# Layer 0 values as three fp32r products, key maxima from a block-diagonal kT_hi, loads issued by SyncE, and another order of steps, in a fused two-layer gated cross-attention kernel

## What is computed

```python
x = x + tanh(g_xattn[0]) * L0_xattn(layernorm(x), ctx)   # 16 heads of 64, keys and values from ctx
x = x + tanh(g_ffn[0])   * L0_ffn(layernorm(x))          # softmax gate, 8 experts of 256x256, threshold 0.1
x = x + tanh(g_xattn[1]) * L1_xattn(layernorm(x), ctx)   # 16 heads of 16, biases
x = x + tanh(g_ffn[1])   * L1_ffn(layernorm(x))          # routed swiglu experts
# x: (64, 256, 256), ctx: (64, 120, 256), all float32

def L0_xattn(x, ctx):
    q, k, v = x @ Wq.T, ctx @ Wk.T, ctx @ Wv.T           # inner size 1024
    attn = softmax(q k / 8)                              # per head, 256 queries x 120 keys
    return (attn @ v) @ Wo.T + bo
```

## Time and profile before

| | |
|---|---|
| median of three runs | 3751.11 us (3750.22 to 3751.85) |
| profiled execution, own time | 3753.66 us |
| its span | 3751.7 us |
| TensorE busy | 3675.7 us, 98% |
| TensorE weight loads | 2990.3 us, 80% |
| VectorE busy | 2420.4 us, 65% |
| ScalarE busy | 1707.0 us, 46% |
| GpSimd busy | 1508.2 us, 40% |
| mean granted TensorE clock | 0.997 |

### The profile page before, as it was taken

The page is one execution under the profiler, slowest core; times in us unless marked ns, Lnnn a source line. Parts: engine busy times, 40 slices in busy tenths (PEclk is TensorE's granted clock), DMA queues, the critical chain, the costliest instruction groups (busy, mean ns, idle before and its releaser), DMA issues.

```text
span 3751.7 us, 96179 instructions
## 1 busy us (share of the span) xinstructions
PE 3675.7 (98%) x34836; PEld 2990.3 (80%) x34836; DVE 2420.4 (65%) x5566; ACT 1707.0 (46%) x3115; POOL 1508.2 (40%) x1589
## 2 busy tenths in 40 slices
...
PEclk9999999999999999999999999999999999999999
...
GB/s 96 11 14 16 11 14 16 11 14 16 11 14 16 11 14 16 11 14 16 11 14 16 11 14 16 11 14 16 11 14 16 11 14 16 11 14 16 11 27 64
DMA packets 58916, 64.83 MB, mean 17 GB/s; under 512 B 5344, under 2 KB 55808, under 8 KB 58240
## 3 DMA queue, kind: packets, MB, share of 16 engines
...
## 4 chain that ended last, share of the span: by engine, by line
PE 77%; POOL 7%; DVE 7%; issue 5%; ACT 2%; POOLq 1%; DVEq 1%; SPq 0%; DMA 0%; ACTq 0%
PE g L834 24%; PE g L840 13%; PE scores L834 10%; PE g L987 6%; PE scores L937 6%; POOL q_lo L608 4%; PE g L1006 3%; PE g L903 3%; PE scores L997 3%; DVE y_nm L1269 3%; POOL kmx L601 2%; PE g L854 2%; PE scores L971 2%; PE scores L941 2%; PE g L914 1%
## 5 line engine op out<-in xcount | busy, mean ns | idle before, releaser
L777 ACT ACTIVATE prob<-scores 120x1024 f32<-120x1024 f32 x512 | 499.6, 1026 | 481.0 <-PE scores L941 444.1
L1330 DVE SCALAR_TENSOR_TENSOR x<-g,lg_w,x 128x256 f32<-128x256 f32 x1024 | 494.5, 483 | 259.9 <-PE g L834 236.1
L834 PE MATMUL g<-ew_hi,yT_hi 128*128 128x512 f32 x1024 | 428.1, 418 | 0.0
L543 POOL TENSOR_TENSOR y_rstd<-y_mv,eps 128x2 f32<-128x2 f32 x128 | 24.9, 195 | 970.5 <-DVE y_mv L1188 970.5
L613 POOL TENSOR_TENSOR q_lo<-an,q_hi 128x512 fp32r<-128x512 f32 x256 | 326.6, 1286 | 210.3 <-ACT q_hi L806 210.3
L834 PE MATMUL g<-ew_lo,yT_hi 128*128 128x512 f32 x1024 | 404.7, 395 | 0.0
L834 PE MATMUL g<-ew_hi,yT_lo 128*128 128x512 f32 x1024 | 404.1, 395 | 0.0
L1269 DVE TENSOR_REDUCE y_nm<-g 128x4 f32<-128x480 f32 x512 | 301.1, 651 | 110.1 <-PE g L914 110.1
L1269 DVE TENSOR_REDUCE x_nm<-g 128x4 f32<-128x480 f32 x512 | 312.4, 653 | 72.3 <-PE g L903 72.3
L543 POOL TENSOR_TENSOR x_rstd<-x_mv,eps 128x2 f32<-128x2 f32 x64 | 12.5, 196 | 835.7 <-DVE x_mv L1188 835.7
L608 POOL TENSOR_TENSOR q_lo<-q_full,q_hi 128x512 fp32r<-128x512 f32 x256 | 324.9, 1291 | 1.1 <-ACT q_full L711 1.1
...
## 6 DMA issues: line engine op xcount, KB each, us to landing
...
ctx_in<-in_ctx ACTq DMA_DIRECT2D x128, 120.0 KB, 2.4
...
```

What stands on the lines that cost most here:

```text
L777: a.activation(prob[:, e].rearrange("p o u s -> p (o u s)"), scores[0:NK, banks, :].rearrange("p o c -> p (o c)"), ACT.Exp, scale=scale).t ...
L834: ins = t_.matmul(out_, lhsT[u], rhs[v], start=first and n == 1, stop=last and n == 3 * len(terms))
L1330: ins = v.scalar_tensor_tensor(out=x1[:, t, :], in0=ring.bank(Y_FFN[j])[:, o * D:(o + 1) * D], scalar=lg_w[:, t, 2 * n + o:2 * n + o + 1], ...
```

## The change

It has six parts.
1. Layer 0 values: wv is kept as a high and a low part, ctxT as fp32 and as a pair; `n_v` uses `products`.
2. `kT_hi` is now block-diagonal itself (two column blocks a pair, zero where the other head is). ScalarE writes its two halves of 64 partitions with one copy each, VectorE subtracts kT_lo in two halves, `n_max` reads kT_hi; `kmx` and its GpSimd product are gone.
3. `n_load` and `p_load` are issued by SyncE from batch 3 (2) on, with waits for what the DMA overwrites.
4. ORDER and ENDS are other lists, and each engine's hardware loop is cut at a step of its own: TensorE ahead of n_maxt 0, VectorE x_out 1, ScalarE y_hi 0, GpSimd x_mul 3, SyncE n_load 0.
5. At the start the splits come as wq, wv, wo, w1 and the experts' weights in four quarters, over three staging areas; the gate's weights are read in place.
6. The routed layer uses other buffers, its gate weights are loaded in halves of 256 KB, one per step m_gu, and the negated mean for GpSimd's normalisation is computed by GpSimd.

The diff, cut to its core (the other ENDS lists and the buffers of part 6 are left out):

```diff
ORDER = (
-    ("n_load", 0), ("x_st", 0), ("x_st", 1), ("y_ffn", 0), ("n_stat", 0), ("y_ffn", 1), ("z_hi", 1), ("y_k", 0),
-    ("y_ffn", 2), ("y_ffn", 3), ("n_norm", 0), ("y_ffn", 4), ("y_ffn", 5), ("x_st", 2), ("x_st", 3), ("y_ffn", 6),
-    ("n_tr", 0), ("y_ffn", 7), ("y_stat3", 0), ("x_sum", 0), ("x_pv", 0), ("x_mul", 0), ("x_mul", 1), ("x_hi", 0),
-    ("x_mul", 2), ("x_mul", 3), ("x_pv", 1), ("x_pv", 2), ("x_hi", 1), ("x_sum", 1), ("x_pv", 3),
-    ("y_tr3", 0), ("z_out", 0), ("x_hi", 2), ("y_v", 0), ("n_ctx", 0), ("y_q", 0), ("x_hi", 3), ("n_k", 0),
-    ("x_out", 0), ("y_max", 0), ("x_out", 1), ("x_out", 2), ("y_max", 1), ("y_res", 0), ("x_out", 3), ("p_stat", 0),
-    ("y_maxt", 0), ("n_q", 0), ("n_k", 1), ("n_q", 1), ("y_maxt", 1), ("n_q", 2), ("p_load", 0),
-    ("p_tr2", 0), ("n_q", 3), ("n_max", 0), ("y_st", 0), ("n_max", 1), ("p_gate", 0), ("n_v", 0), ("p_lg", 0),
-    ("n_res", 0), ("n_maxt", 0), ("y_st", 1), ("n_max", 2), ("n_v", 1), ("n_max", 3), ("p_wt", 0), ("y_pv", 0),
-    ("y_mul", 0), ("y_pv", 1), ("y_mul", 1), ("n_maxt", 1), ("p_ctx", 0), ("p_eb", 0), ("y_hi", 0),
+    ("n_load", 0), ("x_st", 0), ("n_stat", 0), ("x_st", 1), ("y_ffn", 0), ("y_ffn", 1), ("y_ffn", 2), ("n_norm", 0),
+    ("y_ffn", 3), ("y_ffn", 4), ("y_ffn", 5), ("y_ffn", 6), ("y_ffn", 7), ("n_tr", 0), ("x_st", 2), ("z_hi", 1),
+    ("y_stat3", 0), ("x_st", 3), ("x_pv", 0), ("x_sum", 0), ("x_mul", 0), ("x_hi", 0), ("x_sum", 1), ("x_pv", 1),
+    ("x_mul", 1), ("x_mul", 2), ("x_hi", 1), ("x_pv", 2), ("x_pv", 3), ("y_k", 0), ("y_tr3", 0), ("x_hi", 2),
+    ("x_mul", 3), ("z_out", 0), ("x_hi", 3), ("y_q", 0), ("y_v", 0), ("y_res", 0), ("n_ctx", 0), ("x_out", 0),
+    ("y_max", 0), ("n_res", 0), ("x_out", 1), ("x_out", 2), ("y_max", 1), ("x_out", 3), ("n_q", 0), ("y_maxt", 0),
+    ("p_stat", 0), ("n_k", 0), ("n_k", 1), ("n_q", 1), ("n_q", 2), ("y_maxt", 1), ("p_tr2", 0), ("n_q", 3),
+    ("n_max", 0), ("p_gate", 0), ("p_load", 0), ("n_max", 1), ("y_st", 0), ("n_max", 2), ("p_lg", 0), ("n_v", 0),
+    ("n_maxt", 0), ("y_st", 1), ("n_max", 3), ("n_v", 1), ("p_wt", 0), ("y_mul", 0), ("n_maxt", 1), ("y_pv", 0),
+    ("y_pv", 1), ("p_ctx", 0), ("p_eb", 0), ("y_mul", 1), ("y_hi", 0),
 )
...
-        w1_s = pair("w1", [P, 2 * KD * D + KD * NE])
-        wk_s, wv_s = sb("wk_s", [P, KD, INNER]), sb("wv_s", [P, KD, INNER])
+        GATES = KD * NE
+        w1_s = pair("w1", [P, GATES + 2 * KD * D])
+        wv_s = pair("wv", [P, KD, INNER])
+        wk_s = sb("wk_s", [P, KD, INNER])
...
-        gate_s = pair("gate", [P, KD, P])
+            return w1_s[n][:, GATES + KD * D:GATES + 2 * KD * D].rearrange("p (k n) -> p k n", k=KD)
+
+        def gate_s(n, k):
+            return w1_s[n][:, k * NE:k * NE + P]
...
-        kT = pair("kT", [P, NPAIR, NK])
-        kmx, half = sb("kmx", [P, NPAIR, 2, NK], F32R), sb("half", [P, 2])
+        kT_hi, kT_lo = sb("kT_hi", [P, NPAIR, 2, NK], F32R), sb("kT_lo", [P, NPAIR, NK], F32R)
...
+        ctx_nm = sb("ctx_nm", [P, D + T * P])
+        ctx_in, x_nm = ctx_nm[0:NK, 0:D], ctx_nm[:, D:].rearrange("p (t n) -> p t n", t=T)
+        ctxT, ctxT_s = sb("ctxT", [P, KD, NK]), pair("ctxT", [P, KD, NK])
...
-        def run(eng, table, setup=None, setup_x=None):
-
-
-            def one(*batches, setup=None):
-                for name, k, i in steps(*batches):
+        def run(eng, edge, table, setup=None, setup_x=None):
+
+
+            at = ORDER.index(edge)
+
+            def one(*batches, setup=None, part=slice(None)):
+                for name, k, i in steps(*batches)[part]:
                     if name in table:
                         table[name](i, k)
                     if setup and (name, k) in setup:
@@ -407,20 +414,27 @@
             one(None, None, 0, None, None, -1, setup=setup)
             one(0, None, 1, 0, None, 0, setup=setup_x)
             one(1, 0, 2, 1, None, 1)
+            def turn(i, part):
+                one(i, i - 1, i + 1, i, i - 2, part=part)
+
             one(2, 1, 3, 2, 0)
-            with eng.Fori(3, B - 1) as i:
-                one(i, i - 1, i + 1, i, i - 2)
+            turn(3, slice(0, at))
+            with eng.Fori(3, B - 2) as i:
+                turn(i, slice(at, None))
+                turn(i + 1, slice(0, at))
+            turn(B - 2, slice(at, None))
...
-        splits = [(flat(wq), flat(wq_s[0][:]), flat(wq_s[1][:])), (flat(wo), flat(wo_s[0][:]), flat(wo_s[1][:]))]
+        splits = [(flat(a), flat(parts[0][:]), flat(parts[1][:])) for a, parts in ((wq, wq_s), (wv, wv_s), (wo, wo_s))]
         splits += [(w1, w1_s[0][:], w1_s[1][:])]
-        splits += [(ew[:, k, :], ew_s[0][:, k, :], ew_s[1][:, k, :]) for k in range(KD)]
+        splits += [(ew[:, k, cols], ew_s[0][:, k, cols], ew_s[1][:, k, cols])
+                   for k in range(KD) for cols in (slice(0, NE * D // 2), slice(NE * D // 2, NE * D))]
         NSPLIT = len(splits)
-        WQ, WO, W1, EW = 1, 2, 3, 5
-        stage = (prob_rows[:, 0:2].rearrange("p a b c s -> p (a b c s)"), vx1[:])
+        WQ, WV, WO, W1, EW = 1, 2, 3, 4, 8
+        stage = [prob_rows[:, 2 * n:2 * n + 2].rearrange("p a b c s -> p (a b c s)") for n in range(2)] + [vx1[:]]
...
-        AFTER = (max(("n_ctx", 0), ("n_tr", 0), key=in_order.index), ("n_k", 0), ("n_q", 1))
-        AFTER_X = (("x_st", 3), ("x_out", 0), ("x_out", 1), [step for step in ORDER if step[0][0] in "xnp"][-1])
-        STAGES = (0, 1, 0, 1, 1)
-        STAGED = (1, len(wo_blocks), 2, len(wo_blocks) + 1, len(wo_blocks) + 2)
-        STAGE_FREE = (0, 0, 1, 2, 4)
+        AFTER = (max(("n_ctx", 0), ("n_tr", 0), key=in_order.index), ("n_k", 0), ("n_q", 1), ("n_q", 3))
+        AFTER_X = (("x_st", 3), ("x_out", 0), ("x_out", 1), ("x_out", 2), ("x_out", 3), [step for step in ORDER if step[0][0] in "xnp"][-1])
+        STAGES = (0, 1, 0, 1, 2, 2, 2, 2)
+        STAGED = (1, 1, 1 + len(wo_blocks), 3, 1, 2, 3, 4)
+        STAGE_FREE = (0, 0, 1, 2, 0, 5, 6, 7)
...
+            def n_load(i, _):
+                if not early(i, 3):
+                    x_resd.wait(sp, i, 0)
+                    x_normed.wait(sp, i, 0)
+                    sp.dma_start(x_in[:], x_rows[i]).then_inc(x_loaded.sem, 16)
+
+                    ring.full(sp, i - 2, Y_CTX)
+                    sp.dma_start(ctx_in, ctx[i]).then_inc(ctx_loaded.sem, 16)
+
+            def p_load(i, _):
+                if not early(i, 2):
+                    if isinstance(i, int) and i + 1 >= B:
+                        ring.full(sp, i - 1, Y_CTX)
+                    else:
+                        ring.full(sp, i + 1, X_CTX)
+                    sp.dma_start(ctx_in, ctx[i]).then_inc(ctx1_loaded.sem, 16)
...
-            def m_gate_weights(i, e):
-                if e >= 2:
-                    ring.m_full(sp, *M_GU[KD * (e - 2) + 1])
-                sp.dma_start(gu_s[e % 2], gu[e]).then_inc(m_gu_in[e % 2], 16)
+            def m_gate_weights(i, n):
+                e, m = n // KD, n % KD
+                sp.dma_start(gu_s[n % 2], gu[e][:, :, :, m * P:(m + 1) * P]).then_inc(m_gu_in[n % 2], 16)
+
+            def m_gate_next(i, n):
+                if n + 2 < KD * NE:
+                    ring.m_full(sp, *M_GU[n])
+                    m_gate_weights(i, n + 2)
...
+                if minus:
+                    g.tensor_tensor(y_minus[:], mv[:, :, 0], minus_one[:], ALU.mult)
                 done.wait(pool, i, k + 1)
-                if minus:
-                    stats.wait(pool, i, k_stats + 1)
                 g.tensor_tensor(rs[:, 1, :], rs[:, 0, :], neg_half[:, 0:T], ALU.pow).then_inc(done.sem, 1)
...
-            def x_k(i, c):
-                if first(i):
-                    pool.wait_ge(dve_zeroed, 1)
-                x_khi.wait(pool, i, 1 + c)
-                g.tensor_tensor(kmx[:, 4 * c:4 * c + 4, :, :],
-                                kT[0][:, 4 * c:4 * c + 4, :].bitcast(F32).unsqueeze(2).broadcast_to([P, 4, 2, NK]),
-                                half[:].unsqueeze(1).unsqueeze(3).broadcast_to([P, 4, 2, NK]),
-                                ALU.mult).then_inc(x_kmx.sem, 1)
...
-                ring.has_emptied(a.copy(flat(ctxT[:]), ring.bank(X_CTX)[:, 0:KD * NK]), X_CTX)
+                a.copy(flat(ctxT[:]), ring.bank(X_CTX)[:, 0:KD * NK]).then_inc(x_ctx_in.sem, 1)
+                a.copy(flat(ctxT_s[0][:]), ring.bank(X_CTX)[:, 0:KD * NK]).then_inc(x_ctx_in.sem, 1)
...
             def x_k(i, c):
-                hi_of(x_khi, i, X_K[c], 4 * NK, flat(kT[0][:, 4 * c:4 * c + 4, :]))
+                if first(i):
+                    act.wait_ge(dve_zeroed, 1)
+                ring.full(act, i, X_K[c])
+                for o in range(2):
+                    rows = slice(64 * o, 64 * o + 64)
+                    last = a.copy(kT_hi[rows, 4 * c:4 * c + 4, o, :],
+                                  ring.bank(X_K[c])[rows, 0:4 * NK].rearrange("p (m n) -> p m n", m=4))
+                last.then_inc(x_khi.sem, 1)
...
-                ring.to_fill(pe, i, X_K[c], X_CTX)
+                ring.to_fill(pe, i, X_K[c])
```

(30 more changed lines are left out.)

260 lines of the change are left out of this document (128 added, 132 removed).

## The result

The changed kernel takes 3708.93 us (median of four runs, 3704.49 to 3711.03) against 3751.32 us for the kernel before on the same chip: a ratio of 0.9887, 95% interval 0.9875 to 0.99. That is 42 us less; I had forecast 53 less. The profiled execution took 3710.72 us, its span is 3709.0.

A forecast was written before the change was run, and what follows sets the result against it. TensorE's pace, 98% busy, was taken as the bound. Seven terms summed to -0.79 us a turn, x 61 = -48; other batches' values -2, start -4 and +1: -53 from 3751.1, giving 3698 us, range 3655 to 3728.

The forecast's parts named there:

- values: Both n_v steps a batch: six fp32r products replace two fp32 ones, 1.40 us for 1.72, saving 0.64 us a batch.
- n_max 1's stop: Ahead of n_max 1: the stop for ScalarE's q_full goes because kmx no longer delays GpSimd's q_lo, saving 0.21 us a turn.
- one run less: x_st 2 and 3 directly ahead of x_pv: one row-tiled run fewer between full-array products, saving 0.20 us a turn.
- old wait at y_q: Ahead of y_q: the wait for yT_lo, delayed by GpSimd's late q_lo, disappears, saving 0.22 us a turn.
- x_st 0 behind p_eb: TensorE's loop edge leaves p_eb / x_st 0 for ahead of n_maxt 0, covered by queued n_v work, saving 0.20 us a turn.
- new wait ahead of y_q: After z_out: y_v and n_ctx no longer stand ahead of y_q, so it waits for yT_lo, costing 0.25 us a turn.
- new wait around p_gate: p_gate, behind n_q 3 and n_max 0 alone, waits for yT_lo, costing 0.43 us a turn.
- the rule of the Trainium skill: Rival for values: three products replace four passes, a quarter saved, 0.86 us a batch, 3684 us in all; chance 0.03.
- VectorE's or GpSimd's longer lists would swallow the gain: Rivals: VectorE empties banks late, only values pay, 3708 us, chance 0.15; GpSimd makes xn late, unchanged 0.05, slower 0.05.
- there would be no new waits: Rival: ScalarE reaches y_tr3 and p_tr2 earlier, so both new waits vanish, 41 us more saved, 3657 us; chance 0.17.
- The start: First batch: splitting wo after n_q 1 saves 4 of TensorE's 6.2 us stop for q_full; chunked experts' weights cost 1.
- The end: Last stretch: TensorE back to back for 51.8 us, gate weights' loads just fit; no change.

The follow-up runs named there:

- number 1: The kernel after with layer 0's values as fp32 products again, low part of wv left out: 3744.2 us, ratio 0.9979 to the kernel before.
- number 8: The kernel after with x_st 2 and 3 back between y_ffn 5 and y_ffn 6, a row-tiled run of their own: 3718.2 us, ratio 0.9908.
- number 2: The kernel after with TensorE's loop edge back at the start of its list: 3705.6 us, ratio 0.9879 to the kernel before.
- number 5: The kernel before with only TensorE's loop edge moved ahead of n_maxt 0: 3757.8 us, ratio 1.0017.
- number 6: The kernel before with only the new ORDER list of the steady turns: 3792.1 us, ratio 1.0108.
- 9: The kernel before with n_maxt 1 moved ahead of y_pv 1 in the steady turns: 3757.6 us, ratio 1.0011.
- number 3: The kernel after with y_maxt 1 ahead of n_q 2 and n_max 1 ahead of p_gate: 3745.7 us, ratio 0.9981 to the kernel before.
- number 10: The kernel after with the loads of x and the context issued by ScalarE instead of SyncE: 3705.0 us, ratio 0.9876 to the kernel before.
- 7: The kernel before with only the maxima taken straight from a block-diagonal kT_hi, without kmx: 3800.9 us, ratio 1.013.

## Why the prediction was right, and where it was not

The forecast was 3698 us, within 3655 to 3728; it is 3708.9. The loop is right and slightly small (0.88 a turn for 0.79); the 11 us that are missing lie in the start and the end. That the sum of the turn comes out so close is in part luck: of its seven terms three were off by 0.05 to 0.09, one more has another cause, and one holds where it was tested and not from before to after. Point by point, in us a turn, the distances between first products averaged over the steady turns:

| term | predicted | measured | by |
|---|---|---|---|
| values | -0.64 | -0.63 | number 1 |
| n_max 1's stop | -0.21 | -0.30 | y_st 0, 1.13 for 1.43 |
| one run less | -0.20 | -0.19 | number 8 |
| old wait at y_q | -0.22 | -0.31 | n_ctx 0, 0.13 for 0.44 |
| x_st 0 behind p_eb | -0.20 | -0.20 | 0.41 for 0.60 |
| new wait ahead of y_q | +0.25 | +0.24 | z_out 1.74 for 1.50 |
| new wait around p_gate | +0.43 | +0.38 | 0.28 ahead of p_gate, 0.10 ahead of n_max 1 |

The measured terms add up to -1.01, the period fell by 0.88. The difference is the run: number 8 prices it in the new order, but from before to after the stretch from x_st 0 to the end of x_pv and y_k is only 0.06 us shorter (22.36 to 22.30). y_ffn gave 0.44, and n_tr beside a run takes 0.53 for 0.36, y_k behind x_pv 0.99 for 0.81.

- **Values.** Number 1 settles it, by the two paces of the earlier trace rows. By the rule of the Trainium skill (FP8 and Floating Point Precision, TensorE Precision Notes) it would have been 0.86 a batch; the runs do not follow it.
- **The edge: a right number for a wrong cause.** "The loop's edge on TensorE moves ... Gain 0.20" failed as an explanation. The edge costs 0.04 at its old place in the new order (number 2), and moving it alone loses (number 5). The 0.20 were register operations that no queued product covered: behind the branch with the edge there, behind the wait for x_nmT without it. The order removed both, since n_maxt 1 now has y_pv 0 and 1 behind it (numbers 6 and 9). My line "n_maxt 1 is earlier, so x_st 0 cannot wait for x_nmT" had half of the cause in it, priced at nothing.
- **The waits.** y_q and p_gate wait as worked out, for yT_lo, y_q 0.24 us and p_gate 0.28 where 0.43 was forecast. The other 0.10 stands ahead of n_max 1, where the prediction had no stop left; it is the wait for q_full that number 3 laid open. That VectorE's or GpSimd's longer lists would swallow the gain did not happen. The other direction, that there would be no new waits, neither.
- **Loads.** Nothing, as said (number 10).
- **Parts and their sum.** The order alone costs 0.30 and the maxima alone 0.83; together, with fp32 values and the loads and edge of after (number 1), they gain 0.25. They are worth 1.38 us more together than one by one: the order needs GpSimd rid of kmx, and the longer key copies need the order's distance between n_k and y_max. That last price, "about 1 us a turn" with the cover gone, measured 1.21.
- **The start**, predicted at -4 with 1 given back, is the step that failed. The 6.2 us stop is 3.0, but x_st 0 of batch 0 starts at 43.7 us, before at 43.3, so nothing of it arrives; and batch 0 then loses 4.3 us at x_out 1. The turn of batch 1 starts at 90.0 to 96.1 us in the profiles of the kernels with these lists (and at 84.5 to 85.8 in those of before, 5, 7 and 9): 7 to 13 us later than forecast. I had priced the splits of the weights and not walked the new first list, in which x_hi 3 moved behind n_k 0 and n_stat 0. Putting it back brings 1.7 us at a like clock; about 5 us go with the granted clock; the rest no run parts, and number 6 shows that ORDER alone can move the start by 10 us.
- **The end**, predicted at 0, costs 3.4 in the two profiles. "The end is TensorE back to back" was true of before; I had not walked SyncE's new queue, where a load stands behind another's wait.

Open: the rest of the start, and why the granted clock differs at the start and at the end between runs of the same lists. Whether y_q's wait can be had without y_max's was tried in one way only.
